# Last cross attention: GpSimd adds the two halves of its key sums, and TensorE makes one product with ones per head

## The reference, cut to what matters

```
q = split_heads(x @ Wq) * 64 ** -0.5
k, v = split(context @ Wkv)               # each split into heads
k = concat(null_key, k); v = concat(null_value, v)
sim  = einsum('bhid,bhjd->bhij', q, k)
attn = softmax(sim, axis=-1)              # over 1602 keys
out  = einsum('bhij,bhjd->bhid', attn, v)
out  = layer_norm(merge_heads(out) @ Wout) * ln_scale + ln_bias
```

## Time and profile before

| | us |
|---|---|
| median of 3 runs | 4894.95 (4885.61 to 4895.87) |
| the profiled execution's own time | 4905.05 |
| its span, first to last instruction | 4903.2 |
| busy, PE | 4032.0 (82%) |
| busy, DVE | 3202.5 (65%) |
| busy, ACT | 2379.5 (49%) |
| busy, POOL | 1422.2 (29%) |
| from 2781 to 4645 us (the stage of the change): PE, DVE, ACT, POOL busy | 1826.0, 1472.4, 973.3, 1146.1 of 1864.0 |

### The profile page before, as it was taken

How to read it: one execution, slowest core, us unless ns; L and a number is a source line. 1 busy time by engine, 2 the same in 40 slices (tenths; PEclk the granted TensorE clock), 3 DMA queues, 4 the chain that set the end, 5 groups by cost and what they waited for, 6 DMA issues and landing times. The chain is left out here.

```text
span 4903.2 us, 76709 instructions
## 1 busy us (share of the span) xinstructions
PE 4032.0 (82%) x28627; PEld 2455.7 (50%) x28631; DVE 3202.5 (65%) x5519; ACT 2379.5 (49%) x4513; POOL 1422.2 (29%) x1147
## 2 busy tenths in 40 slices
PE   3399999679279984588887799999999999999854
PEld 2133333358233332366665466666666666666532
DVE  3499999522277746533333388787878787878757
ACT  3288888424178861133332255555555555555420
POOL 0200000000300000011110066566656665666510
PEclk7599999779689985577777899999999999999977
DMA  5322221000065400000000100000000000000001
GB/s 158 66 45 52 45 50 42 1 20 19 17 97 82 67 2 13 14 0 0 0 0 8 54 1 14 1 14 14 1 14 1 14 1 14 1 1 1 1 19 35
DMA packets 119690, 122.86 MB, mean 25 GB/s; under 512 B 21264, under 2 KB 97648, under 8 KB 118992
## 3 DMA queue, kind: packets, MB, share of 16 engines
q1 hardware_dynamic: 119240, 118.20, 11.3%
q10 hardware_dynamic: 144, 0.52, 0.0%
HBM read 102.95 MB, written 15.73 MB: 24 GB/s over the span
## 5 line engine op out<-in xcount | busy, mean ns | idle before, releaser
L832 DVE TENSOR_REDUCE att_peak.1<-psS 128x1 f32<-128x512 f32 (+1 forms) x1024 | 580.7, 633 | 94.5 <-PE psS L702 94.4
L2634 POOL TENSOR_TENSOR key_sums_0.1<-key_sums_0.1,prob_0.1 128x512 f32<-128x512 f32 x256 | 402.4, 1572 | 29.0 <-POOL key_sums_0.1 L2629 0.4
L801 ACT ACTIVATE att_probT.1<-psT 128x512 f32<-128x512 f32 (+1 forms) x682 | 368.8, 568 | 74.8 <-PE psT L731 33.1
L2634 POOL TENSOR_TENSOR key_sums_1.1<-key_sums_1.1,prob_1.1 128x512 f32<-128x512 f32 x256 | 386.2, 1509 | 28.7 <-POOL key_sums_1.1 L2634 0.4
L2473 ACT COPY prob_0.1<-psS 128x1024 f32<-128x1024 f32 (+1 forms) x224 | 203.7, 954 | 323.4 <-PE psS L2372 323.3
L832 DVE TENSOR_REDUCE att_peak.2<-psS 128x1 f32<-128x512 f32 (+1 forms) x512 | 266.7, 569 | 137.6 <-PE psS L702 135.7
L702 PE MATMUL psS<-key_stack.1,query_stack.1 64*128 64x512 bf16 (+1 forms) x1024 | 272.2, 387 | 94.6 <-DMA key_stack.1<-key_parts 48.2
L2473 ACT COPY prob_1.1<-psS 128x1024 f32<-128x1024 f32 (+1 forms) x224 | 203.7, 954 | 296.3 <-PE psS L2372 296.3
L748 PE MATMUL psM<-att_probT.1,quad_values.1 128*9 128x256 f32 (+1 forms) x3840 | 306.0, 391 | 19.4 <-issue 19.4
L2543 DVE TENSOR_TENSOR att_highest.1<-att_highest.1,prob_1.1 128x1024 f32<-128x1024 f32 (+1 forms) x160 | 280.7, 1754 | 53.7 <-ACT prob_1.1 L2473 46.4
L2543 DVE TENSOR_TENSOR att_highest.1<-att_highest.1,prob_0.1 128x1024 f32<-128x1024 f32 (+1 forms) x160 | 271.1, 1695 | 56.5 <-ACT prob_0.1 L2473 49.9
(11 more groups left out here) (675 smaller groups left out, 9043.8 us busy)
## 6 DMA issues: line engine op xcount, KB each, us to landing
key_stack.1<-key_parts SPq DMA_DIRECT2D x384, 58.0 KB
key_stack.2<-key_parts SPq DMA_DIRECT2D x96, 200.1 KB
ctx_rows.1<-in_ctx_dram SPq DMA_DIRECT2D x8, 1536.0 KB
key_parts<-split_parts.1 SPq DMA_DIRECT2D x8, 1200.8 KB, 5.7
ctx_keys_0.1<-in_ctx_dram SPq DMA_DIRECT2D x4, 768.0 KB
ctx_keys_1.1<-in_ctx_dram SPq DMA_DIRECT2D x4, 768.0 KB
query_stack.1<-query_parts SPq DMA_DIRECT2D x192, 16.0 KB
ctx_values_0.1<-in_ctx_dram SPq DMA_DIRECT2D x4, 768.0 KB
```

Source lines behind the costliest of these rows:

```text
L801: last = self.k.nc.scalar.activation(probs[:, blks[0]:blks[-1] + 1, :].rearrange("p b q -> p (b q)"), bank[0:w, 0:len(blks) * S], ACT.Exp)
L832: self.k.nc.vector.tensor_reduce(self.peak[:, 2 * h + s, c:c + 1], self.score_bank[m % 3][:, 0:w], AX_X, ALU.max).then_inc(self.peak_done. ...
L2634: nc.gpsimd.tensor_tensor(acc, acc, own[:, h, c * BANK:(c + 1) * BANK], ALU.add).then_inc(self.summed.sem, 1)
```

## The change

GpSimd gets one more add for each head, behind the tail add: the first half of `key_sums` plus the second, 128x256, in place. `pe_total` then makes one product for each head in place of two. The counts of the semaphore `summed` follow (7 steps for each head and not 6, 14 for each turn and not 12).

```diff
@@ pe_total
-        pe.wait_ge(*self.summed(12 * (i + 1)))
+        pe.wait_ge(*self.summed(14 * (i + 1)))
         if i + 1 < self.TURNS:
             pe.wait_ge(*self.lowered(8 * (i + 2)))
-        for part in range(2):
-            for h in range(2):
-                last = nc.tensor.matmul(self.peaks[h * self.HD:(h + 1) * self.HD, 0:S], self.ones[:], self.acc[i % 2][:, h, part * S:(part + 1) * S],
-                                        start=(part == 0), stop=(part == 1))
+        for h in range(2):
+            last = nc.tensor.matmul(self.peaks[h * self.HD:(h + 1) * self.HD, 0:S], self.ones[:], self.acc[i % 2][:, h, 0:S],
+                                    start=True, stop=True)
         last.then_inc(self.totalled.sem, 1)
@@ act_keep
-            act.wait_ge(*self.summed(12 * (i - 2) + 6 + max(s, 1)))
+            act.wait_ge(*self.summed(14 * (i - 2) + 7 + max(s, 1)))
@@ pool_sums
-        summed = 12 * i + 6 * h
+        summed = 14 * i + 7 * h
...
         tail = acc[0:self.NULL, 0:S]
         nc.gpsimd.tensor_tensor(tail, tail, own[0:self.NULL, h, 6 * BANK:6 * BANK + S], ALU.add).then_inc(self.summed.sem, 1)
+        pool.wait_ge(*self.summed(summed + 6))
+        nc.gpsimd.tensor_tensor(acc[:, 0:S], acc[:, 0:S], acc[:, S:2 * S], ALU.add).then_inc(self.summed.sem, 1)
```

More of the change, by code:

```diff
@@ L2305, in finish @@
             sig.passed(8 * T)
-        self.summed.passed(12 * T)
+        self.summed.passed(14 * T)
         for sig in (self.totalled, self.inverted, self.out_done):
```

## The result

The changed kernel takes 4904.23 us (median of 14 runs, 4894.44 to 4913.63) against 4895.24 for the kernel before in the same runs: a ratio of 1.0022, with a 95% interval from 1.0012 to 1.0031. It is slower by 9 us, though TensorE has 256 matmul instructions less. The profiled execution took 4910.59 us, 5.5 more than that of before.

What follows compares the result with a forecast made beforehand. TensorE looked like the bound, VectorE nearly level, its raises alternating with GpSimd's adds. Turn kinds gave +17.5 - 7.6 + 2.1 - 2.9 = +9.1; with -1.0 and +1.1, +9.2 on 4894.95: 4904 us, range 4893 to 4917.

Steps and rivals of the forecast that it cites:

- Who bounds: TensorE busy 1826.0 of 1864.0 us, but VectorE's divide and peak arrive nearly together with it.
- plain turns: 33 turns without context blocks or output product: raise 4 waits for the later add 2; 28.20 against 27.67 us, +0.53 each.
- The shared interface and its prices: GpSimd's adds and VectorE's raises run one at a time; after waiting, a raise needs 1.08 us, an add of 512 1.13.
- The place of raise 4: Head 1's adds start 0.80 us later; the effect depends on where raise 4 arrives among them, for each kind of turn.
- last blocks: 7 turns with the last context blocks (pair 6): raise 4 waits longer for add 3; +0.30 us each.
- output product: 7 turns with an output product (pair 2): raise 4 meets add 4, not add 5; -0.41 us each.
- The full-context turns: 14 turns (pairs 4 and 5): raise 4 meets add 3, not add 4; -0.54 us each.
- The first and the last turn: First turn and last before the drain: raise 5 gets in between the adds, some 0.5 us back each, -1.0 together.
- The drain: Stage's last turn, waiting for GpSimd alone: two new adds, 1.60 us, less 0.54 of TensorE, +1.1.
- The new adds hide: Rival: new adds don't disturb VectorE, so plain turns gain 0.27 us and full context none; 4879 us, chance 7%.
- Slower by a place lost: Rival: raise 4 falls behind add 4 again in full-context turns, another +17 us, 4921; chance 10%.
- The clock: Rival: more TensorE idle time in plain turns lowers its granted clock of 1.00, costing tens of us; chance 3%.

Runs made afterwards that it cites:

- The products alone: Against the kernel before: TensorE makes one product with ones a head, GpSimd adds nothing new, second halves left out of totals; 4886.28 against 4901.77 us, ratio 0.9971.
- the adds alone: Against the kernel before: GpSimd makes both new adds into a tile nobody reads, TensorE keeps its four products a turn; 4921.34 against 4901.77 us, ratio 1.0041.
- the fill: Changed kernel with a GpSimd fill of 128x740, reading nothing, for each new add, second halves left out; 4906.08 us against 4900.8 of the kernel before, ratio 1.0012.
- the late adds: Two kernels against the one before: new adds in one instruction behind head 1's tail add, ratio 0.9966; or behind head 1's add 5 and tail add, 0.9967.
- 150 elements: Changed kernel with head 0's new add 150 wide, not 256, into a spare tile, second halves left out; 4914.96 us against 4900.8 of the kernel before, ratio 1.0035.
- the place chosen by the kind of turn: Against the kernel before: head 0's new add between the heads in 14 full-context turns, elsewhere behind head 1's add 5; 4882.4 against 4901.77 us, ratio 0.9962.

## Why the prediction was right, and which of its terms were off

- *Who bounds.* It said that TensorE and VectorE arrive nearly together in plain turns, so that TensorE's saving gives at most 0.27 there. The products alone gave 0.28.
- *The shared interface and its prices.* Shown by the earlier trace rows and confirmed: the adds alone, without any change on TensorE, brought the plain turns to 28.19, against 28.20 by the arithmetic. Raise 4 ended 1.09 us after the add (3512.19 to 3513.28), where the prediction had 1.08, and a raise that no add held took 1.22; the new add took 0.72 where nothing held it, and not the 0.55 of the prediction's lower end. VectorE's instructions with an input in PSUM were not held up in the trace of the kernel before: of its 64 reciprocals (L2570), the 42 with a GpSimd instruction beside them for more than half of their time took 1.74 to 1.76 us, and the 8 with none 1.74 to 1.76; the divide (L2578) took 0.40 in 42 turns with one beside it and 0.40 to 0.43 in 22 without; a lowering of 1024 (L2564) took 1.21 or 1.22 in 192 cases with one and in 190 without. That the price is paid by raise 4 behind a late old add, and not by the new add, is shown by the fill and by the late adds.
- *The place of raise 4.* Plain +0.53, measured +0.51; last blocks +0.30, measured +0.26; output product -0.41, measured -0.43 (medians over the turns of a kind).
- *The full-context turns.* The sign was right, the size was not: -0.54 forecast, -0.44 measured. The term that failed is TensorE's saving. The prediction halved the 1.08 us of eight instructions. Those 1.08 include the run of the last ones, over which the next product is already issued. From the first product with ones to the next product with values it was 0.91 us (3516.09 to 3517.00), and now it is 0.48. The next product before, then both lines of the changed kernel:

```profile
3517.00 0.60 PE L2418 MATMUL psT<-prob_1.1,values_1.1 66*64 66x256 f32 x4
...
3512.74 0.65 PE L2402 MATMUL psO<-key_sums_1.1,att_ones.1 128*64 128x256 f32 x4
3513.22 0.60 PE L2417 MATMUL psT<-prob_1.1,values_1.1 66*64 66x256 f32 x4
```

  So 0.43 is saved and not 0.54. It shows where TensorE bounds, above all in the full-context turns, whose sum came out at -6.4 and not -7.6.
- *The first and the last turn.* -1.0 was forecast, -1.7 and -2.5 were measured. The raise that gets in between the adds gives 1.2 us by itself, and not 0.5, and the rest of VectorE's turn follows. In the first turn it is raise 5 (2.78 us before, 1.56 now); in the last it is raise 4, which stood behind both the tail add and head 1's add 1. That makes 1.7 us on VectorE in each: the peak is issued at T + 24.88 and now at T + 23.16 in the last. TensorE's saving has no part in the first turn, which is 23.17 with the adds alone too. The other 0.8 of the last turn is the clock: its products with values took 3.47 us at a granted clock of 0.54, and now 2.64 at 0.71 (1.95 at 1.00). Raise 4 and these products in the last turn, before and then now:

```profile
4606.29 2.38 DVE L2543 TENSOR_TENSOR att_highest.1<-att_highest.1,prob_1.1 128x1024 f32<-128x1024 f32 x1
4613.06 3.47 PE L2418 MATMUL psT<-prob_0.1,values_0.1 128*64 128x256 f32 x16 [4.91 <-DVE att_outT.3 L2578]
...
4609.03 1.21 DVE L2542 TENSOR_TENSOR att_highest.1<-att_highest.1,prob_1.1 128x1024 f32<-128x1024 f32 x1
4614.09 2.64 PE L2417 MATMUL psT<-prob_0.1,values_0.1 128*64 128x256 f32 x16 [3.62 <-DVE att_outT.3 L2577]
```

- *The drain.* +1.1 was forecast, +3.4 measured. GpSimd is the engine that is waited for, as forecast (the wait before the last total grew from 0.23 to 2.24 us), but 1.35 of it is the clock: the output product took 3.81 us at 1.00 and now 5.16 at 0.72. Whether the change brings that about is open. The stretch was 30.6 us with the products alone, without any new add, and its output product 5.44; in all eight kernels of the experiments it was 30.6 to 33.5, in one execution each, so the kernel before is the only one with 28.6. Before, then now:

```profile
4640.79 3.81 PE L2358 MATMUL psT<-wout.1,att_outT.3 128*128 128x128 f32 x32 [1.98 <-DVE att_outT.3 L2578]
...
4640.02 0.65 PE L2402 MATMUL psO<-key_sums_1.1,att_ones.1 128*64 128x256 f32 x4 [2.24 <-POOL key_sums_1.1 L2639]
...
4643.08 5.16 PE L2358 MATMUL psT<-wout.1,att_outT.3 128*128 128x128 f32 x32 [1.98 <-DVE att_outT.3 L2577]
```

- *The sum.* +9.2 forecast, +8.2 for the stage in the trace, +9.0 by the medians of the runs. Part of that closeness is luck: the terms were off by -1.0 (plain turns), +1.2 (full context), -3.2 (first and last) and +2.3 (drain), the two other kinds by -0.1 or -0.2, and most of it cancels.
- *The rivals.* "The new adds hide" falls with the adds alone (+20 us). "Slower by a place lost" did not happen here, but it is real: with 150 elements add 4 gets ahead of raise 4, and the full-context turns are 30.52, 0.48 above the kernel before. The clock is 1.00 over the stage, and lower only at its end (1.00 from 2781 to 4600 us of the changed kernel, 0.93 from 4600 to 4645).

## What to carry to other kernels

Where GpSimd and VectorE hold each other up in every turn, as the adds and the raises do here (a raise issued during an add ended 1.08 or 1.09 us behind it), look in the timeline at which of them is issued first at the instruction that the turn's end depends on. GpSimd had 321 us of waiting to spare, and still 0.80 us of delay in its adds made the plain turns 0.51 longer, which TensorE's saving alone had made 0.28 shorter. A delay can as well gain: the full-context turns became 0.44 shorter, where the saving alone gave 0.03. Put added GpSimd work where no raise and no peak is due behind it, and work it out for each kind of turn: here the edit cost 9 us with head 0's add between the heads, gained 14 to 16 with all new work behind head 1's add 5, and 19 with the place chosen by the kind of turn.

## What the runs showed of the hardware

- A blocked raise of 1024 ended 1.08 or 1.09 us after GpSimd's add in 248 of 250 cases of the kernel before, where it took 1.22 in the 70 cases with no add in front of it, as if 0.14 of it could pass while it waits. One issued 0.06 to 0.09 us ahead of the add's end still took 1.22 or 1.23 (the 14 full-context turns of the changed kernel).
- The other way round, an add of 512 issued while a raise of 1024 stood ended 1.12 to 1.15 us after the raise in 224 of 226 cases of the kernel before, where it took 1.26 to 1.28 with no raise and no peak in front.
- A waiting raise got its turn between two GpSimd adds where the second reads what the first has written, and did not in the two cases in which it reads nothing of it. In the trace of the kernel before, such a dependent add was issued 0.08 us or more after the one before had ended, and the raise came in between. The independent one (head 1's add 1 behind head 0's tail add) was issued 0.03 or 0.04 before that end, in all 64 turns. A raise was waiting there in two turns only, the first and the last, and ended behind both: head 1's add 1 in the first turn of the kernel before was issued at 2826.76, the tail add ended at 2826.80, and raise 5, which had been waiting, stayed behind both. In the first turn of the changed kernel raise 5 got in between the tail add and the new, dependent add, and raises 4 and 5 together took 2.89 us where they had taken 4.11. The kernel before, then the changed one:

```profile
2824.99 4.11 DVE L2543 TENSOR_TENSOR att_highest.1<-att_highest.1,prob_1.1 128x1024 f32<-128x1024 f32 x2 [0.54 <-ACT prob_1.1 L2473]
```

```profile
2820.44 2.89 DVE L2542 TENSOR_TENSOR att_highest.1<-att_highest.1,prob_1.1 128x1024 f32<-128x1024 f32 x2 [0.54 <-ACT prob_1.1 L2472]
```

- GpSimd's f32 adds took 0.45 us for 150 elements in a row, 0.72 for 256, 1.03 for 400 and 1.27 for 512, on 128 partitions.
